# Gate and up products of a feed-forward stage by Strassen's scheme, with token pairs as the outer loop and memory placed by hand

## What is computed

```python
def _L0_ffn_ref(x, w_gate, w_up, w_down):       # x 4 x 512 x 512, w_gate and w_up 512 x 2048
    h = silu(einsum('bsh,hi->bsi', x, w_gate)) * einsum('bsh,hi->bsi', x, w_up)
    h_sparse = _sparsify_2to4(h)                # of each 4 neighbours the 2 largest in magnitude
    return einsum('bsi,ih->bsh', h_sparse, w_down)
```

## Time and profile before

| | |
|---|---|
| three runs | 1091.79, 1092.13, 1092.42 us; median 1092.13 |
| span of the profiled execution, first to last instruction | 1090.9 us |
| busy over the span | PE 1037.0 (95%), DVE 738.5 (68%), ACT 486.3 (45%), POOL 294.7 (27%) |
| TensorE, 600 to 1000 us | 100.0% busy, granted clock 1.00 |
| DVE and ACT, 600 to 1000 us | 54.6% and 23.6% busy |
| POOL, 700 to 1000 us | 0% busy |

### The profile page before, as it was taken

How to read it: one execution, slowest core, us unless ns; L and a number is a source line. 1 busy time by engine, 2 the same in 40 slices (tenths; PEclk the granted TensorE clock), 3 DMA queues, 4 the chain that set the end, 5 groups by cost and what they waited for, 6 DMA issues and landing times.

```text
span 1090.9 us, 18063 instructions
## 1 busy us (share of the span) xinstructions
PE 1037.0 (95%) x6022; PEld 839.6 (77%) x6023; DVE 738.5 (68%) x1769; ACT 486.3 (45%) x905; POOL 294.7 (27%) x496
## 2 busy tenths in 40 slices
...
PEclk9999999999999998999999999999999999999998
...
GB/s 260 237 200 204 78 199 200 197 83 188 199 117 117 207 143 77 79 77 164 175 162 61 1 1 40 39 39 1 1 77 12 27 0 33 45 1 1 39 27 89
DMA packets 55216, 106.18 MB, mean 97 GB/s; under 512 B 6240, under 2 KB 8288, under 8 KB 55136
## 3 DMA queue, kind: packets, MB, share of 16 engines
...
## 4 chain that ended last, share of the span: by engine, by line
PE 57%; DVE 2%; ACT 1%; issue 0%; DMA 0%; POOL 0%; POOLq 0%; DVEq 0%
PE f_bank L53 55%; PE f_bank L1714 1%; PE f_bank L1722 1%; PE f_bank L1793 1%; PE f_bank L1738 0%; DVE ln_stats L1104 0%; DVE rows_kept L2150 0%; ACT rows_kept L1132 0%; DVE h L2116 0%; DMA rows<-sorted_dram 0%; DVE rows_kept L2139 0%; DVE h L2056 0%; DVE rows_kept L1111 0%; POOL out L1660 0%; ACT fsg L1936 0%
## 5 line engine op out<-in xcount | busy, mean ns | idle before, releaser
L1896 ACT ACTIVATE fsg<-f_bank 128x512 f32<-128x512 f32 x64 | 38.2, 598 | 295.6 <-PE f_bank L53 289.2
L2056 DVE TENSOR_TENSOR h<-f_bank,fsg 128x512 f32<-128x512 f32 x64 | 44.2, 691 | 181.6 <-PE f_bank L53 181.4
L714 ACT ACTIVATE probs<-bank,nmax 128x384 f32<-128x384 f32 (+3 forms) x256 | 131.7, 549 | 21.4 <-DVE nmax L899 19.3
L883 DVE CUSTOM_DVE_ANT_0 bank<-bank,mask 128x384 f32<-128x384 f32 (+3 forms) x256 | 122.9, 502 | 13.8 <-PE bank L510 13.0
L521 PE MATMUL bank<-ident,probs 128*128 128x128 f32 x640 | 108.7, 284 | 24.6 <-DVE pt_lo L908 10.7
L1137 POOL TENSOR_SCALAR ln_var<-ln_mv 128x1 f32<-128x1 f32 x39 | 8.9, 229 | 438.8 <-DVE ln_mv L1106 437.4
L908 DVE TENSOR_TENSOR pt_lo<-bank,pt_hi 128x512 f16<-128x512 f32 (+1 forms) x192 | 114.7, 598 | 16.7 <-ACT pt_hi L724 16.4
L724 ACT ACTIVATE pt_hi<-bank 128x512 f16<-128x512 f32 (+1 forms) x192 | 104.9, 546 | 23.5 <-PE bank L521 22.9
L53 PE MATMUL bank<-x_hi,w_qk 128*128 128x512 f32 x256 | 101.5, 414 | 6.7 <-DVE x_lo L913 6.3
L53 PE MATMUL f_bank<-wd_hi,hs_lo 128*128 128x512 f32 x256 | 100.0, 391 | 0.0
L53 PE MATMUL f_bank<-wd_lo,hs_hi 128*128 128x512 f32 x256 | 99.9, 390 | 0.0
...
## 6 DMA issues: line engine op xcount, KB each, us to landing
...
```

Of the source, the lines that this page charges most:

```text
L714: ins = act.activation(probs[u % RP][:, at:at + cols(r)], S[u % SR][:, at:at + cols(r)], ACT.Exp, bias=nmax[:, r, c:c + 1])
L883: dve.tensor_tensor_reduce(out=S[u % SR][:, at:at + cols(r)], in0=S[u % SR][:, at:at + cols(r)], in1=mask[:, T - cols(r):T], scale=1.0, sc ...
L1896: act.activation(fsg[v % 2][:, :], GB[v % 2][:, :], ACT.Silu).then_inc(s_sg, 1)
L2056: dve.tensor_tensor(h[r % 2][:, j, :], UB[v % 2][:, :], fsg[v % 2][:, :], ALU.mult).then_inc(s_h, 1)
```

## The change

Gate and up of one slice are one 2 x 2 block product: the weight blocks are (up, gate) by two halves of the 512 input features, the token blocks are two halves of the features by two row blocks of 512 tokens. Strassen's scheme makes it from seven products, each of half the depth (2 x 3 matmuls of 128 x 512), where the direct way has eight. A **round** L handles two slices ("a", "b") of a pair of row blocks, so it has 14 products; a chunk of a token pair has two rounds, a pair has 8, and there are 2 pairs: 16 rounds. The token pair is the outer loop now, so the weights are loaded and cut once per pair, twice in all. What each engine gets:

- TensorE: 14 products of 6 matmuls a round, in the order of `ORDER`; sums of products that share an output are made in PSUM by accumulating onto a bank after ScalarE has copied it (`s_copied`). The down product of block d = L - 2 follows each round from 2 to 13; rounds 0, 1 and 14 have none, and behind round 15 stand four. It uses three banks.
- ScalarE: six copies of banks into SBUF a round, four Silus in SBUF, the high halves of seven pairs of weight blocks (`weight_hi`), magnitudes, high halves of the kept values, and in even rounds four high halves of down weights.
- VectorE: six additions of a bank to a copied sum (`add_product`), four gating products, four low halves of weight pairs (`weight_lo`), the same comparison, count and choice, `kept_lo`, `add_up`.
- GpSimd: four sums of weight blocks a round (`weight_sums`), three low halves of weight pairs, and in even rounds four low halves of down weights (`down_lo`).
- The seven token blocks of a pair (three of them sums on VectorE, and one more in place) are cut into halves at the start of the pair; for the second pair this stands around the end of round 7 (`LB`) and the start of round 8.
- Raw weights have one buffer (1 MB): those of round L + 1 are loaded when the low halves of round L are done. The high and low halves have one buffer too, group by group behind the products that read them.
- All 16 rounds are written out; there is no hardware loop in this stage.
- The stage's tiles are put at fixed addresses in one arena.

The diff, cut to what the steps below speak of:

```diff
+    ORDER = ("1a", "1b", "2a", "5a", "6a", "6b", "5b", "7a", "7b", "2b", "4a", "4b", "3a", "3b")
+    BLOCK = {"1": "B11", "2": "B21", "5": "T1", "6": "T2", "7": "T3", "4": "T4", "3": "B22"}
+    after_round = {L: [L - 2] for L in range(2, ROUNDS - 2)}
+    after_round[ROUNDS - 1] = [ROUNDS - 4, ROUNDS - 3, ROUNDS - 2, ROUNDS - 1]
+        VB, FB, PB, YB = bank[0:2], bank[3], (bank[5], bank[2]), (bank[4], bank[6], bank[7])
...
+            def weights_in(L):                                   # SyncE
+                if L > 0:
+                    sp.wait_ge(*wlo_ready(L - 1, GROUPS - 1))
+                    sp.wait_ge(*wlo_ready(L - 1, GROUPS - 2))
+                for i in range(2):
+                    j = 2 * (L % 2) + i
+                    sp.dma_start(raw[:, i, 0:4 * P], up[chunk(L), j]).then_inc(s_wraw, 16)
+                    sp.dma_start(raw[:, i, 4 * P:8 * P], gate[chunk(L), j]).then_inc(s_wraw, 16)
...
+            def product(L, name):                                # TensorE
+                if AT[name] % 2 == 0:
+                    pe.wait_ge(*wlo_ready(L, AT[name] // 2))
+                if L % (2 * NCH) == 0 and name[1] == "a":
+                    pe.wait_ge(s_xl, xcount(p, BLOCK[which]))
+                opens = which in "125"
+                if which == "1":
+                    to = VB[i]
...
+                        pe.wait_ge(s_h0, 2 * (L - 1) + i + 1)
+                elif which == "2":
+                    to = FB
+                    if name == "2b":
+                        pe.wait_ge(s_ad, added(L, "11a"))
+                    elif L > 0:
+                        pe.wait_ge(s_ad, added(L - 1, "11b"))
+                elif which == "5":
+                    to = PB[i]
+                    if L > 0:
+                        pe.wait_ge(s_ad, added(L - 1, f"12{name[1]}"))
+                elif which == "3":
+                    to = PB[i]
+                    pe.wait_ge(s_ad, added(L, f"22{name[1]}"))
+                else:
+                    to = VB[i]
+                    pe.wait_ge(s_cp, copied(L, {"6": "1", "7": "6", "4": "7"}[which] + name[1]))
+                for k in range(HALF):
+                    for a, b in ((0, 0), (0, 1), (1, 0)):
+                        ins = pe.matmul(to[:, :], aw[a][:, g, n, k * P:(k + 1) * P], x[b][:, k, :], ...)
...
+            def down_product(d, ts=range(RW)):
+                    if t == 0:
+                        pe.wait_ge(s_hl, 2 * (d + 1))
+                        pe.wait_ge(s_dlo, J * (s + 1))
+                    n = RW * d + t
+                    if n >= len(YB):
+                        pe.wait_ge(s_acc, n - len(YB) + 1)
...
+            def round_(L):                                       # ScalarE
+                soon = L >= 3 and odd and more
+                copy(L, "1a")
+                copy(L, "1b")
+                if odd:
+                    magnitudes(s, 0, 0)
+                elif L > 0 and L != LB + 1:
+                    magnitudes(s - 1, 1, 0)
+                    magnitudes(s - 1, 1, 1)
+                copy(L, "6a")
+                copy(L, "6b")
+                if soon:
+                    weight_hi(L + 1, 0)
+                    weight_hi(L + 1, 1)
+                if L >= 2 and not odd:
+                    down_hi(s - 1, range(2))
+                copy(L, "7a")
+                copy(L, "7b")
+                silu(L, 0, 0)
+                if L >= 2:
+                    kept_hi(L - 2)
+                if L >= 2 and not odd:
+                    down_hi(s - 1, range(2, J))
+                if L == LB + 1:
+                    magnitudes(s - 1, 1, 0)
+                    magnitudes(s - 1, 1, 1)
+                for g in range(2 if soon else 0, 4) if more else ():
+                    weight_hi(L + 1, g)
+                silu(L, 0, 1)
+                for g in (4, 5) if more else ():
+                    weight_hi(L + 1, g)
+                silu(L, 1, 0)
+                silu(L, 1, 1)
+                if more:
+                    weight_hi(L + 1, 6)
...
+            def round_(L):                                       # VectorE
+                add_product(L, "11a")
+                if L == LB + 1:
+                    token_lo(1, "T3")
+                    token_lo(1, "T4")
+                    token_lo(1, "B22")
+                early(L)          # even L: compare(L - 1); round 8: compare, count, choose of 6
+                add_product(L, "22a")
+                add_product(L, "22b")
+                if more:
+                    weight_lo(L + 1, 0)
+                add_product(L, "11b")
+                gated_first(L, 0)
+                if more:
+                    weight_lo(L + 1, 2)
+                gated_first(L, 1)
+                if L >= 2:
+                    kept_lo(L - 2)
+                add_product(L, "12a")
+                add_product(L, "12b")
+                if more:
+                    weight_lo(L + 1, 4)
+                gated_second(L, 0)
+                gated_second(L, 1)
+                if more:
+                    weight_lo(L + 1, 6)
+                if more:
+                    behind(L)     # compare (odd L), count and choose of L - 1, add_up of L - 2 between
```

964 lines of the change are left out of this document (562 added, 402 removed).

## The result

The changed kernel takes 1159.23 us (median of 4, 1152.48 to 1161.38) against 1091.96 us of the kernel before on the same chip: a ratio of 1.0605, 95% interval 1.0574 to 1.0636. It is 67 us slower; 11 us slower was forecast. The profiled execution is the fastest of the four (span 1150.7 us); the others show a granted clock of 0.953 to 0.960 in the place of its 0.961.

The account below looks back on a forecast made before the run. TensorE was taken to bound the kernel: 43.5 us less work against 54.7 us of new waits gave +11.2, a span of 1102.1 us and a forecast time of 1103 us; range for 8 in 10: 1080 to 1124.

Parts of the forecast that it names:

- The gain: TensorE's last stage: gate and up take 1344 matmuls in place of 1536, 192 x 0.2268 = 43.5 us less.
- Even rounds: Rounds 2, 4, 6, 10, 12: TensorE waits 3.4 + 1.0 us each for h_lo, 22.0 us, between 17 and 28.5.
- The walk: One round followed through the in-order queues: TensorE waits for h_lo 3.4 us in even rounds, 0.9 in odd ones.
- The port: VectorE's two-SBUF-input instructions and GpSimd's exclude each other late in a round: 1.0 us more in even rounds, 0.6 in odd.
- Odd rounds: Rounds 3, 5, 9, 11, 13: TensorE waits 0.9 + 0.6 us each for h_lo, 7.5 us, between 4.5 and 13.
- The start: First rounds: waits for a token block (1.3 us), round 1's weights (2.5) and round 2's selection backlog (0.9), 4.7 us together.
- Change of pair: Rounds 7 and 8: waits for evictions (1.5 us), 3a (1.5) and h_lo (9.1), together 12.1 us, between 10.5 and 14.
- rounds 14 and 15: No down product between these rounds: 2.0 us of TensorE waits, between 1.3 and 3.
- tail: Four down products behind round 15: with three banks for four tiles, row sums free banks late, 4.1 us.
- The clock: TensorE's matmuls run at 1.2 GHz behind a long idle gap: 2.3 us, charged once, for round 8.
- rival 3: Strict alternation on the port, and the clock falls in even rounds too: 86.7 us of waits, 1135 us; chance 0.1.
- Rival 4: GpSimd becomes the bound, its 11.6 us a round and VectorE's 15 us excluding each other: about 1110 us; chance 0.15.

Follow-up runs that it names:

- e2_light: Changed kernel with GpSimd's weight sums and weight low halves on 8 of 256 columns from round 1 on, down-weight halves whole: 1118.42 us, 1.0232 of the kernel before.

## Why the prediction was wrong, point by point

- **The gain** was right: 192 matmuls fewer at 0.227 us, 43.5 us.
- **Even rounds**, 22.0 forecast: 4.31, 5.75, 5.31, 4.95 and 4.94 us, 25.3, inside the bounds. The walk was right to a tenth for rounds 10 and 12, as e2_light showed (3.44 us against 3.4). The port costs 1.0 to 1.5 us a round by the difference to e2_light, where 1.0 was taken and 2.3 was the bound; in round 10 that is the two h_lo, 2.37 us in e2_light and 1.5 more in the changed kernel. In rounds 4 and 6 landings add some 0.9 us (4.32 and 4.29 in e2_light): in round 6 the chain of waits passes 9.74 us over wd_raw's, against the 5.3 of the earlier trace rows for as many bytes. The likely cause is the scatters, which the prediction left out; no run moves them alone.
- **Odd rounds**, 7.5 forecast: 2.0 to 2.8 us each, 11.2; 4.8 in e2_light. The port costs 1.1 to 1.8 us each, and 0.6 was taken.
- **The start**, 4.7 forecast: 12.3. The product of round 1 and that of round 2 waited 3.73 and 5.79 us, where 2.5 and 0.9 were forecast; choosing beside GpSimd's sums took 6.7 us in the place of 2.50. The port stood in the prediction for h_lo only, and not where selection and sums meet.
- **Change of pair** 15.1 for 12.1, **rounds 14 and 15** 3.4 for 2.0, **tail** 5.5 for 4.1: all a little short. The first two are 10.8 and 2.1 in e2_light, so GpSimd's load is their reason. The tail is 5.6 there; but its counts run beside the down low halves, which e2_light leaves whole (1.51 us for 0.42 in both kernels), so the port is likely in it too.
- **The clock**, 2.3 forecast: 28.5. This is the step that failed: "I charge it once, for round 8; the even rounds' gaps (about 4.4 us) have no row, between 0 and 2.3 each." I took the low end, zero, for all of them. The runs showed near the high end: behind the even rounds' gaps of 4.3 to 5.8 us stood 8 to 11 slow matmuls, 1.7 to 2.4 us a gap and 10 in sum. Six of the 13 groups, moreover, stood behind gaps of rounds 1, 2, 3, 11, 13 and 15 for which the prediction had no clock term at all; so even the 7 x 2.3 = 16.1 us of rival 3 are too low. In the profiled span 48.6 us were missed: 26.2 by the clock, 7.6 by the start, some 13 by the other terms, mostly the port's share, and 2 that no term holds. The other 7 us are that the median execution lies so much above the profiled one.
- **Rivals.** What happened was the mechanism of rival 3 (strict alternation, clock in the even rounds), given 1135 and a chance of 0.1, and it was larger still: in even rounds the port cost 1.0 to 1.5 us, under the 2.3 of its strict alternation, and the clock far more than its 16.1 us. Against it stood only that no gap of that length is in the trace of before; a missing row was read as a reason. The Trainium skill, TensorE: Matmul & The Clock Gate, section "HAM oscillation — how this bites in real kernels", warns that idle gaps between a kernel's matmuls bring the clock down again. The runs agree (28.5 us), and the prediction didn't weigh it. The Trainium skill, SBUF — State Buffer, section "SBUF: two separate sides", says of a VectorE instruction with two SBUF inputs and one of GpSimd that reads SBUF that whichever starts first holds the port to its end and the other waits. That was borne out at more places than I used it: a count of 0.42 us took 1.51 beside a sum of 1.3 to 1.5. Rival 4 was discarded because sums "end near 3" us of a round; they ended at 12.7 in round 6, and GpSimd's load turned out to be worth 41 us in this order.
- The range, 1080 to 1124, left out the end of rival 3 and was so too narrow on the slow side. Direction and place of most waits were right.
